# Four dense layers and a small model in one block without loops, with the readout beside the last dense layer

## What is computed

```python
x = layernorm(x + x @ masked(W0).T)                       # layer A
x = layernorm(x + x @ W1.T + b1 + lora(x, batch))         # layer B
x = layernorm(x + small_model(x))                         # M and C
x = layernorm(x + x @ W3.T + b3 + experts(x, routing))    # layer D
```

## Time and profile before

| | |
|---|---|
| median of three runs | 1999.91 us (1998.6 to 2013.88) |
| profiled execution | 2012.65 us, span 2010.9 us |
| mean granted TensorE clock | 0.918 of 2.4 GHz |
| TensorE busy | 1827.5 us, 91% of the span |
| VectorE, ScalarE, GpSimd busy | 1030.3, 631.4, 538.4 us |
| DMA | 207.28 MB, 103 GB/s mean |

### The profile page before, as it was taken

The page is one execution under the profiler, slowest core; times in us unless marked ns, Lnnn a source line. Parts: engine busy times, 40 slices in busy tenths (PEclk is TensorE's granted clock), DMA queues, the critical chain, the costliest instruction groups (busy, mean ns, idle before and its releaser), DMA issues. The chain is left out here.

```text
span 2010.9 us, 25961 instructions
## 1 busy us (share of the span) xinstructions
PE 1827.5 (91%) x8103; PEld 1408.7 (70%) x8103; DVE 1030.3 (51%) x1877; ACT 631.4 (31%) x900; POOL 538.4 (27%) x681
## 2 busy tenths in 40 slices
PE   1899999968999999999659999998996799999998
PEld 0688788855787878788547766664553588878887
DVE  5356422235555455543246777745865555555542
ACT  1232333333223232322125555542322323232221
POOL 3011111123000000000068988932543300000000
PEclk9999999977999999999859999995755899999999
DMA  4322262223322223222140000004753433333321
GB/s 178 129 84 84 105 245 86 104 94 120 106 103 100 103 101 103 100 84 79 45 165 1 1 1 1 1 1 170 241 197 136 133 126 130 136 123 118 129 93 65
DMA packets 78796, 207.28 MB, mean 103 GB/s; under 512 B 10041, under 2 KB 23609, under 8 KB 77772
## 3 DMA queue, kind: packets, MB, share of 16 engines
q1 hardware_dynamic: 57580, 135.96, 20.2%
q10 hardware_dynamic: 21088, 69.74, 8.6%
HBM read 129.24 MB, written 76.42 MB: 102 GB/s over the span
## 5 line engine op out<-in xcount | busy, mean ns | idle before, releaser
L259 PE MATMUL A_ps_out<-wall,A_x_hi 128*128 128x512 f32 x512 | 201.9, 394 | 12.2 <-DVE A_x_lo L501 8.8
L259 PE MATMUL B_ps_out<-wall,B_x_hi 128*128 128x512 f32 x512 | 207.3, 405 | 0.0
L259 PE MATMUL D_ps_out<-wall_d,D_x_hi 128*128 128x512 f32 x512 | 204.0, 398 | 0.0
L260 PE MATMUL B_ps_out<-wall,B_x_hi 128*128 128x512 f32 x512 | 201.6, 394 | 0.0
L261 PE MATMUL B_ps_out<-wall,B_x_lo 128*128 128x512 f32 x512 | 201.6, 394 | 0.0
L260 PE MATMUL D_ps_out<-wall_d,D_x_hi 128*128 128x512 f32 x512 | 201.3, 393 | 0.0
L261 PE MATMUL D_ps_out<-wall_d,D_x_lo 128*128 128x512 f32 x512 | 201.2, 393 | 0.0
L260 PE MATMUL A_ps_out<-wall,A_x_hi 128*128 128x512 f32 x512 | 201.0, 393 | 0.0
L261 PE MATMUL A_ps_out<-wall,A_x_lo 128*128 128x512 f32 x512 | 200.9, 392 | 0.0
L566 DVE BATCH_NORM_STATS2 A_stats<-A_row 128x6 f32<-128x512 f32 x64 | 44.4, 694 | 198.9 <-ACT A_row L411 197.5
L643 POOL TENSOR_SCALAR B_var_eps<-B_mean_var 128x1 f32<-128x1 f32 x32 | 6.1, 190 | 465.2 <-DVE B_mean_var L574 465.2
(11 more groups left out here) (282 smaller groups left out, 3667.0 us busy)
## 6 DMA issues: line engine op xcount, KB each, us to landing
A_x_in<-in_x_t SPq DMA_DIRECT2D x32, 512.0 KB, 3.4
x_scratch<-A_row ACTq DMA_DIRECT2D x32, 512.0 KB, 2.6
B_x_in<-x_scratch SPq DMA_DIRECT2D x32, 512.0 KB, 3.9
x_scratch<-B_row ACTq DMA_DIRECT2D x32, 512.0 KB, 2.6
C_x_in<-x_scratch SPq DMA_DIRECT2D x32, 512.0 KB, 4.0
x_scratch<-C_row ACTq DMA_DIRECT2D x32, 512.0 KB, 3.4
D_x_in<-x_scratch SPq DMA_DIRECT2D x32, 512.0 KB, 4.2
out<-D_row ACTq DMA_DIRECT2D x32, 512.0 KB, 2.6
```

Source lines behind the costliest of these rows:

```text
L259: pe.matmul(ps_out[h][:], x_hi[:, s, k], walls[par][:, 0, k, cols], start=(k == 0), stop=False)
L260: pe.matmul(ps_out[h][:], x_hi[:, s, k], walls[par][:, 1, k, cols], start=False, stop=False)
```

## The change

The kernel is one block without hardware loops; all waits count up through the whole program, and each tensor has a fixed place in SBUF. Steps are numbered through: A has s = 0 to 31, B 32 to 63, D from B_END = 64 to 95.

- **Start.** The first three tiles of A are multiplied chunk by chunk while the mask is still worked on (`first_products`).
- **A.** The second half of A makes the 16 weight parts of B's first batch, one per tile. PSUM pairs alternate. ScalarE evacuates.
- **B.** As before, with two parts a tile for batches 1 to 3. The tables of the small model are made beside the tiles of its last batch and stay in SBUF.
- **Small model.** Eight more steps of stages a and b make the last layernorm; its high and low parts are stored to DRAM. In turns 6 to 32 all 32 tiles of B's result are loaded, VectorE adds the readout's bias to them (`add_shared`, two adds of 128x512 a tile) and they are stored back.
- **Readout.** Batch 0 is read out in turns 34 to 38. The tiles of batches 1 to 3 are read out in the steps of D one batch ahead, two in each of the steps j = 2 to 5, and that batch's router follows in j = 6 and 7.
- **D.** No part is made beside the tiles of the batch before. At a batch's start its 16 parts are made in line with its first two tiles: the first tile uses a part as soon as it is there, the second four parts later (LAG). All low parts are made by GpSimd. There are two places for w_in and two for a_in.
- The shift is made by ScalarE, the negative mean by VectorE, the root by GpSimd.

The core of it (lines of the kernel before with -, of the one after with +):

```diff
-        RAW = 6
-        def steps(eng, step):
-            with eng.Fori(0, TILES // BODY) as turn:
-                for j in range(BODY):
-                    step(turn, j)
+LAG = 4
+C_TURN = {34: (0,), 35: (1,), 36: (2, 3), 37: (4, 5), 38: (6, 7)}
+C_STEP = {2: (0, 1), 3: (2, 3), 4: (4, 5), 5: (6, 7)}
...
+            # SyncE
+            def load_part(n):
+                at_least(sp, a_hi_ready, n - 1)
+                at_least(sp, a_lo_ready, n - 1)
+                sp.dma_start(a_in[:rank, n % 2], a_from[:, k * P:(k + 1) * P]).then_inc(a_loaded[n % 2], 16)
+                if n >= 2:
+                    sp.wait_ge(w_hi_ready, n - 1)
+                    low_parts(sp, n - 2)
+                sp.dma_start(w_in[:, n % 2], w_from[k][:, o * HALF:(o + 1) * HALF]).then_inc(w_loaded[n % 2], 16)
+            for b in range(BATCHES):
+                p, n, c = B_END + TPB * b, PARTS * (BATCHES + b), TPB * (b + 1)
+                for i in range(2, PARTS):
+                    load_part(n + i)
+                    if i == 6:
+                        load_c(c)
+                        load_z(c)
+                    if i == 8:
+                        load_x(p + 2)
...
+            # TensorE, start
+            for k in range(KC):
+                if k + 2 < KC:
+                    spread_blocks(k + 2)
+                first_products(k)
+            # TensorE, D
+                for i in range(PARTS + LAG):
+                    if i + 2 < PARTS:
+                        weight_part(n + i + 2)
+                    if i < PARTS:
+                        pair_part(p, i)
+                    if i >= LAG:
+                        pair_part(p + 1, i - LAG)
...
+            # ScalarE, D
+                for i in range(PARTS):
+                    if i + 2 < PARTS:
+                        split_a(n + i + 2)
+                    weight_hi(n + i)
...
+            # GpSimd, D
+                for i in range(PARTS):
+                    weight_lo(n + i)
```

More of the change, by code:

```diff
@@ L1 @@
[L1 removed]
+from contextlib import ExitStack
 import concourse.bass as bass
@@ new lines, in x_slot, with before_in_slot, out_bank, part_place @@
+def x_slot(s):
+    return s if s < FIRST else (s - FIRST) % 2
+def before_in_slot(s):
+    return s - FIRST if s < FIRST + 2 else s - 2
+def out_bank(s, h):
+    if s < FIRST:
+        return 2 * s + h
+    if s < A_END:
+        return 2 * ((s - FIRST) % 2) + h
+    return 5 + h if in_pair(s) and s % TPB == 1 else h
+def part_place(n):
+    u = n % PARTS
+    k, o = u % KC, u // KC
+    return n // PARTS, k, o, o == k * P // HALF
+def diagonals(n):
+    return sum(part_place(i)[3] for i in range(n + 1))
@@ L206, in load_parts @@
[L206 to L227, removed]
[L228 to L236 removed]
+            def load_w0(k):
+                sp.dma_start(mask_in[:, k], a["mask_t"][k]).then_inc(mask_loaded[k], 16)
+                sp.dma_start(w0_in[:, k], a["w0_t"][k]).then_inc(w0_loaded[k], 16)
@@ new lines, in product @@
+            def product(s, half, chunks=range(KC)):
+                if chunks[0] == 0:
+                    if half == 0:
+                        pe.wait_ge(hi_ready, s + 1)
+                        pe.wait_ge(lo_ready, s + 1)
+                    bank_free(s, half)
+                if A_END <= s < B_END and s % TPB == 0:
+                    n = PARTS * batch_of(s) + KC * (half + 1)
+                    pe.wait_ge(w_hi_ready, n)
+                    low_parts(pe, n - 1)
+                wall = wall_x if s < A_END else walls[batch_of(s)]
+                for k in chunks:
+                    last = terms(s, half, k, wall)
+                if chunks[-1] == KC - 1:
+                    last.then_inc(mm_done, 1)
@@ new lines, in reduce_total, with router_logits @@
+            def reduce_total(batch):
+                pe.wait_ge(g_ready, FCH * MLP_END)
+                pe.wait_ge(consts, 9 + P // 32)
+                for half in range(2):
+                    pe.wait_ge(totalled[half], (TPB - 1) * (batch + 1))
+                for k in range(KC):
+                    last = pe.matmul(ps_q[:, k:k + 1], total[:, k * P:(k + 1) * P], token_weight[:],
+                                     start=True, stop=True)
+                last.then_inc(q_done, 1)
+            def router_logits(batch):
+                pe.wait_ge(q_taken, batch + 1)
+                for k in range(KC):
+                    last = pe.matmul(ps_l, q[:, k:k + 1], rw[:, k], start=(k == 0), stop=(k == KC - 1))
+                last.then_inc(l_done, 1)
@@ new lines, in router_exp @@
+            def router_exp(batch):
+                act.wait_ge(shifted, batch + 1)
+                act.activation(chance[:], logits[:], ACT.Exp).then_inc(exp_done, 1)
+            w0_hi(0)
+            split_x(0)
+            w0_hi(1)
+            split_x(1)
+            split_x(2)
+            for k in range(2, KC):
+                w0_hi(k)
+            evacuate(0, 0)
+            split_x(FIRST)
+            evacuate(0, 1)
+            evacuate(1, 0)
+            evacuate(1, 1)
+            normalise(0)
@@ new lines, in _ @@
+            for k in range(2, KC):
+                mask(k)
+            for s in range(B_END):
+                root(s)
+                if s == 9:
+                    pool.wait_ge(r2_ready, 1)
+                    pool.tensor_tensor(r_inv[:], r2_safe[:], minus_half[:], ALU.pow).then_inc(r_inv_ready, 1)
+            order = [("d", rotate_back(0)), ("d", rotate_back(1)), ("b", rotate(0)), ("a", root1), ("b", rotate(1)),
+                     ("e", root2)]
+            for turn in range(TURNS):
+                turn_of(order, turn)
+                for c in C_TURN.get(turn, ()):
+                    root_c(c)
@@ L1908 @@
+            root(D_END - 1)
 def kernel(**inputs):
```

2941 lines of the change are left out of this document (1471 added, 1470 removed).

## The result

The changed kernel takes 2141.43 us (median of four, 2140.0 to 2143.6), the kernel before beside it 2002.26: a ratio of 1.0685, interval 1.0639 to 1.0732. It is slower by 6.9%. The direction was forecast; 2026 us and the range up to 2085 were too low.

What follows compares the result with a forecast made beforehand. PE's matmul count was taken to bound the main stages, with idle time between them. D's first part at 1353, plus 676 for D and 8 to the last store, made 2037; 2026 us on the median, range 1935 to 2085.

Steps and rivals of the forecast that it cites:

- A's tiles at 10.88 us each: A's other 29 tiles: products at D's tile time, 315.5 us, plus some 13 for 16 weight parts, again 329.
- B's preparation at nothing: B's last batch: table preparation hides because DVE is busy in half of B; 10 us if that cover fails.
- the adds at +17: Small model: bias adds exclude POOL's work, turns of 10.1 and 11.5 us, 280 against 263; bounds 0 and +50.
- the readout's turns by DVE's work and 7 us of waits: Batch 0's readout, turns 34 to 38: DVE's 6.85 us plus 3.6 a tile; turns make 73, with waits 80.
- the loads between D's parts at +5: D's batch starts: x, cx and z loads delay a_in, +5 us in batches 0 to 2, +2 in the last.
- The chain of 5.2 us a part: D's batch starts: w issue, a_in landing, split, high and low part in series through SP; 4.7 to 5.5, taken 5.2.
- B's start: End of A: three tiles to 78, 329 for the others and 2 between; B starts at 409, not 458.2.
- DVE and POOL block each other and loads delay the chain: Rival, small model and readout turns: waiting adds hold scans, +40, with late landings +16; 2082 on the median; 18%.
- 1.2 GHz in the paced parts costs only at the edges: D's paced parts: PE's 32.6 us of work in 84, even doubled at 1.2 GHz, stays under the chain.
- the slots alone set the pace: Rival, D's parts: a always in time, two slots give 3.2 us a part; 1908 us on the median; 12%.

Runs made afterwards that it cites:

- shortening one link by 0.6 us: D's low parts made by VectorE (0.69 us each) instead of GpSimd (1.28), against the changed kernel: 2103.5 us, ratio 1.0422 to the kernel before.
- the adds apart: Changed kernel with one of a tile's two bias adds moved ahead of the turn's last addition to h: 2118.7 us, ratio 1.0539 to the kernel before.
- Moving one link: Changed kernel with ScalarE normalising a readout tile one turn later, behind that turn's first square: 2129.7 us, ratio 1.0556 to the kernel before.
- the a-first order: Changed kernel with D's a(i+3) load issued before the wait for w(i+2)'s place in SyncE's queue: 2008.2 us, ratio 0.9998 to the kernel before.

## Why the prediction had the direction and the chain right, and the time wrong

The forecast sum was 2037 us of span, the profile shows 2139: 102 more. The steps that failed, in the order of the kernel: A's tiles at 10.88 us each, B's preparation at nothing, the adds at +17, the readout's turns by DVE's work and 7 us of waits, and the loads between D's parts at +5. They are some 8, 18, 34, 18 and 17 us of the 102. The chain of 5.2 us a part, which the forecast was built on, was right, and breaking it takes the whole loss against the kernel before away; it is not what the forecast missed.

| step | forecast | measured |
|---|---|---|
| first three tiles end | 78 | 79.6 |
| B starts | 409 | 418 |
| B lasts | 505 | 523 |
| turns with two, four adds | 10.1, 11.5 | 10.58, 12.86 |
| 27 turns with adds | 280 | 313.6 |
| turns with a readout | 10.5, 10.5, 14, 14, 14 | 15.7, 19.3, 19.8, 19.4, 14.8 |
| turns 33 to 38, all with waits | 80 | 97.6 |
| D's first part | 1353 | 1431 |
| part to part in D | 5.2 | 5.2, with a load between 6.5 to 8.5 |
| first to last low part of a batch | 72.8 + 5, last 72.8 + 2 | 84.1, 83.1, 82.5, 76.8 |
| D | 684 | 708 |

- **The chain through SyncE** was right, and it is shown and not only argued: the 5.2 us stand in the trace, breaking the chain gave 135 us, and shortening one link by 0.6 us gave 38 to 40.
- **"Loads between: +5"** was too small. With 72.8 for the chain itself (13 x 5.2 and 5.2), 83 leaves 10 a batch and 4 in the last, 17 us more in all of the 24 by which D was too long. Two of the three cx loads bring two z loads with them, and then three issues of 0.4 us and their transfers stand before a_in.
- **"I cost it at nothing (10 us if that cover fails)"**, the preparation in B, failed in its mechanism. DVE is busy in half of B, but its pause lies ahead of splitting y and the work stood behind it: some 20 us in B, and 31 to 34 with what followed. Moving the work ahead of the pause gave them back. A mean share of busy time said nothing of the place of the pause.
- **"+17" for the adds** measured 50. POOL's 8.69 and two adds made 10.07 us a turn; this let the adds use up POOL's idle time of 9.73 - 8.69 = 1.04 us a turn. In the changed kernel POOL is busy 9.6 us in a turn of 10.58 and still idle for 1.0, waiting for what ACT makes from the scaled z, and that scaling stands behind the adds. So their cost comes on top of the turn. Another place for one of the two adds doesn't change that: with the adds apart the turn is 10.72 us. Four adds then leave PE idle for 2.5 us, and in most cases the clock was lower in the turn behind, which no term had. The rival "DVE and POOL block each other and loads delay the chain", with +40 and up to 2082 us, was nearer than the forecast, and still 59 us too low; it had 18%.
- **"DVE does 6.85 + 3.6 a tile" for the readout's turns** failed too. I summed DVE's work and added 7 us of waits for all of them; it is a chain over DVE, POOL, ACT and PE, and five turns took 89 us, not 63. Moving one link gave 12 to 14; how much of the rest is a chain and how much DVE's work was not tested and stays open.
- **B's start** was 9 us late, 1.6 of it from the first three tiles. The forecast took A's other 29 tiles at 10.88 us, 315.5 in all, where the row for these very tiles, without a part beside them, has 329.84. That row and 16 x 0.68 make 341; measured are 338.6. So the parts cost no more than D's rows gave, and the product time carried over from D was what was too small. Why a tile of A takes longer was not tried.
- **The clock.** I wrote that 1.2 GHz in the paced parts costs only at the edges. In D PE's busy time went from 561.4 to 481.7 us for as many instructions when the parts came quickly, and its idle time from 147 to 40. How much of the 80 us of busy time the waits would have covered anyway no run shows.
- The rival "the slots alone set the pace" was wrong for this kernel, and near the truth for it with a_in moved: it had 3.2 us a part, the run has 3.0 to 3.4. It took 119 us off the forecast (1908 on the median); the run took 135 off the measured time and stays at 2008, since the other losses are still in it.

## What to carry to other kernels

When a load with a short wait is queued behind one with a long wait, they share the long one: write down for each queue which wait stands in front, and follow one part round until it meets itself. Here that was worth 135 us. Before work is put "where the engine has time", find on the timeline where its pause lies in the order of the queue; work at the far end of that pause costs in full. And put added work in even portions: here a turn that was 2.3 us longer than its neighbours was followed in four of five cases by one at a lower clock. Last, where a row exists for the very tiles that a sum needs, take it, and not a time carried over from another stage.

## What was not expected of the hardware

- A pause of PE of 2.5 us in one turn of the small model was followed in three cases by a turn at a clock of 0.82 to 0.86, 1.7 to 3.3 us longer; in another, with the same pause, by one at 1.00 and 10.57 us (1135.57 to 1146.14). A pause of 1.85 us (in 1001.86 to 1015.15) was followed by one at 0.69 and 14.47 us.
- Two 128x512 adds from SBUF took 2.38 us beside two rotations on GpSimd, which then took 3.41: 5.8 us in all for work that takes 1.38 and 2.54 alone. Each engine lost 0.9 to 1.0 us. Of the two adds one took 0.68 us and the other 1.78, and each rotation 1.72 instead of 1.27.
- A load of 64 KB landed 1.9 us after its issue ahead of the others and 2.5 to 3.3 behind one of 256 KB; over D of the changed kernel it was 1.9 to 4.6, and in the a-first order ScalarE waited up to 5.6 us for one.
